# Demodulation as four side-by-side products and a fold, with woven experts and spread weight pieces

## What is computed

```python
ys = y * scale                                    # scale = 1/sqrt(512)
d = rsqrt(einsum('bi,io->bo', ys * ys, weight * weight) + EPS)
x = x + einsum('bsi,io->bso', x * ys[:, None, :], weight) * d[:, None, :]

shared = silu(xf @ w1) * (xf @ w3) @ w2           # hidden size 1024
s = sigmoid(concat([xf, tf]) @ router_W)
_, topk_idx = top_k(s + router_bias, 2)           # gates from s, normed over the two
h = gelu(einsum('nc,ech->enh', xf, W1e), approximate=False)
y = einsum('enh,ehc->enc', h, W2e)                # 8 experts, hidden size 512
out = x + (shared + einsum('ne,enc->nc', combine, y)) / 3
```

## Time and profile before

| | us |
|---|---|
| time, median of 3 runs | 1148.37 |
| lowest and highest of them | 1056.49, 2671.32 |
| time of the profiled execution | 1060.37 |
| its span, first to last instruction | 1058.6 |
| PE busy | 1031.7 |
| DVE busy | 505.7 |
| ACT busy | 292.0 |
| POOL busy | 332.0 |

### The profile page before, as it was taken

One profiled execution on the slowest core, in us unless ns is written; L12 is line 12 of the kernel. 1 busy time (PEld: TensorE's weight loads), 2 busy tenths in 40 slices (PEclk: granted clock), 3 DMA queues, 4 the chain that ended last, 5 costly groups with the idle time before them and its releaser, 6 DMA issues.

```text
span 1058.6 us, 14641 instructions
## 1 busy us (share of the span) xinstructions
PE 1031.7 (97%) x4712; PEld 842.4 (80%) x4712; DVE 505.7 (48%) x833; ACT 292.0 (28%) x461; POOL 332.0 (31%) x390
## 2 busy tenths in 40 slices
PE   9999999999999999999999998999999999999996
PEld 7888788787888888888888886788788787778874
DVE  4555556668323333243222215555555555555553
ACT  3222442322212212222121113332333233223321
POOL 0000000001223434343323301555455545545543
PEclk8999999999999999999999999999999999999998
DMA  5666688778877677886824777999779999999964
GB/s 171 199 215 223 239 285 260 261 274 278 273 238 263 193 268 241 264 276 201 291 79 108 211 226 193 218 226 221 152 139 191 225 220 226 221 219 222 230 120 80
DMA packets 133146, 228.61 MB, mean 216 GB/s; under 512 B 28912, under 2 KB 83840, under 8 KB 124992
## 3 DMA queue, kind: packets, MB, share of 16 engines
q1 hardware_dynamic: 60256, 144.05, 42.9%
q0 software_dynamic: 31360, 64.12, 26.7%
q10 hardware_dynamic: 41472, 19.68, 8.1%
HBM read 112.85 MB, written 98.38 MB: 200 GB/s over the span
## 4 chain that ended last, share of the span: by engine, by line
PE 69%; DMA 17%; issue 4%; DVE 4%; SPq 2%; POOL 1%; ACT 1%; ACTq 1%; POOLq 0%; DVEq 0%
PE banks L539 11%; PE banks L540 10%; PE banks L541 10%; PE banks L477 6%; PE banks L479 6%; PE banks L478 6%; DMA we_d<-ehl 6%; DMA we<-we_d 4%; PE banks L491 3%; PE banks L493 3%; PE banks L492 3%; PE banks L416 3%; PE banks L417 2%; PE banks L418 2%; DMA xs_d<-xrow,sadr 2%
## 5 line engine op out<-in xcount | busy, mean ns | idle before, releaser
L477 PE MATMUL banks<-xh,w 128*128 128x512 f32 x512 | 199.6, 390 | 0.6 <-DVE xl L738 0.6
L478 PE MATMUL banks<-xl,w 128*128 128x512 f32 x512 | 199.2, 389 | 0.0
L479 PE MATMUL banks<-xh,w 128*128 128x512 f32 x512 | 199.2, 389 | 0.0
L1200 POOL DMA_INDIRECT out<-ys,slot x71 | 124.6, 1754 | 187.2 <-DVE ys L1098 98.0
L807 DVE SCALAR_TENSOR_TENSOR gm<-sil,banks 128x512 f32<-128x512 f32 x64 | 43.9, 686 | 236.3 <-ACT sil L620 236.3
L1091 DVE TENSOR_TENSOR hidtl<-hidt,hidth 128x512 fp32r<-128x512 f32 x71 | 49.1, 692 | 173.8 <-ACT hidth L697 173.8
L539 PE MATMUL banks<-we,hidth 128*128 x284 | 113.6, 400 | 10.6 <-issue 9.0
L1186 POOL DMA_DIRECT2D xg<-xs_d x136 | 100.1, 1106 | 60.6 <-DVE xgt L1072 49.0
L620 ACT ACTIVATE sil<-banks 128x512 f32<-128x512 f32 x64 | 38.1, 595 | 281.8 <-PE banks L479 281.7
L539 PE MATMUL banks<-we,xgth 128*128 x284 | 111.3, 392 | 3.0 <-issue 3.0
L477 PEld LDWEIGHTS banks<-xh,w 128*128 128x128 f32 x512 | 96.1, 188 | 20.9 <-issue 1.1
(11 more groups left out here) (173 smaller groups left out, 1519.1 us busy)
## 6 DMA issues: line engine op xcount, KB each, us to landing
we_d<-ehl SPq DMA_DIRECT2D x32, 1024.0 KB, 7.3
we<-we_d SPq DMA_DIRECT2D x48, 512.0 KB, 6.0
hturn<-hid ACTq DMA_DIRECT2D x284, 64.0 KB
xg<-xs_d POOLq DMA_DIRECT2D x136, 128.0 KB
eraw<-expert_w SPq DMA_DIRECT2D x32, 512.0 KB, 5.6
x1t_d<-x1t SPq DMA_DIRECT2D x8, 1024.0 KB, 8.8
xin<-x1t_d SPq DMA_DIRECT2D x8, 1024.0 KB, 9.0
x_d<-x1tok SPq DMA_DIRECT2D x32, 256.0 KB, 6.3
```

The source lines that it names most:

```text
L477: pe.matmul(ps[hc % 2][:, :], w_hi, xh[:, j, c, :], start=(c == 0), stop=False)
L478: pe.matmul(ps[hc % 2][:, :], w_hi, xl[:, j, c, :], start=False, stop=False)
L479: last = pe.matmul(ps[hc % 2][:, :], w_lo, xh[:, j, c, :], start=False, stop=(c == DC - 1))
L1200: pool.indirect_dma_start(out[:, :], IO(slot[:, t, 0:1], 0), ys[:, t % RING, :], None, compute_op=ALU.add).then_inc(added[t % 2], 16)
```

## The change

**Beginning.** The sixteen products of 4 columns become four products of 512 columns: the weights are now the squared modulation of one chunk, widened from 4 to 32 columns with zeros, and the squared weight matrix streams through. The four chunks go to four groups of 32 columns of the array and leave their partial sums in four groups of 32 partitions. DVE copies the 128 x 512 result out of PSUM, and four products of 4 columns with a 0/1 matrix `fold` add the four groups and turn the result. The fold stands in the last chunk of `first_linear`, behind eight of its twelve products. `cnd` is loaded by ACT's queue, ahead of the x loads, and no more by POOL's.

```diff
@@ tiles
+        modwide = sb("modwide", [DC, Q], FP32, 168)
+        modsq = modwide[:, :, 0:BATCH]
+        fold = sb("fold", [BATCH], FP32, 168.5)
+        dpart = sb("dpart", [D], FP32, 170)
-        hturn = sb("hturn", [RING, SUB, P], FP32, 160)
+        hturn = sb("hturn", [RING, SUB, P], FP32, 128)
-        hidth = sb("hidth", [2, DC, P], FP32R, 132)
+        hidth = sb("hidth", [2, DC, P], FP32R, 160)
@@ tensor, demodulation
+                for c in range(DC):
+                    last = pe.matmul(dpart_ps[c * Q:(c + 1) * Q, :], modwide[:, c, :], w0sq[:, c, :], start=True, stop=True)
+                last.then_inc(dpart_done, 1)
+
+            def demodulation_sum():
+
+                pe.wait_ge(dpart_moved, 2)
                 for o in range(DC):
-                    for c in range(DC):
-                        last = pe.matmul(misc_ps[:, o * BATCH:(o + 1) * BATCH], w0sq[:, c, o * P:(o + 1) * P], modsq[:, c, :],
-                                         start=(c == 0), stop=(c == DC - 1))
+                    last = pe.matmul(misc_ps[:, o * BATCH:(o + 1) * BATCH], dpart[:, o * P:(o + 1) * P], fold[:, :], start=True, stop=True)
                 last.then_inc(misc_done, 1)
@@ vector
+            dve.wait_ge(small_in, 64)
+            dve.tensor_reduce(fold[:, :], ident.rearrange("p (c b) -> p b c", c=DC)[:, 0:BATCH, :], AX.X, ALU.add).then_inc(dpart_moved, 1)
             for c in range(DC):
                 scaled_low(1, c)
-            dve.wait_ge(small_in, 64)
+                if c == 1:
+                    dve.wait_ge(dpart_done, 1)
+                    dve.tensor_copy(dpart[:, :], dpart_ps).then_inc(dpart_moved, 1)
```

```diff
     if isinstance(n, int) and n < 2:
-        half, m = HC // 2 * n, hc
-    elif hc % 2 == 0:
-        half, m = HC // 4 * (n + 2), hc // 2
+        steps, half = ((1, 3, 5, 7), (0, 2, 3, 5))[n], 2 * n
     else:
+        steps, half = (0, 1, 3, 4, 6, 7), 3 * n - 2
+    if hc not in steps:
         return None
+    m = steps.index(hc)
```

```diff
@@ tensor
             pe.wait_ge(tables_done, 3)
+            look_up(0)
+            up(NBLK - 1, HC - 1, 1)
+            down(NBLK - 1, HC - 2)
             pe.wait_ge(gm_done, HC * NBLK - 1 + 2)
-            look_up(0)
+            matmul1(0)
             down(NBLK - 1, HC - 1)
             pe.wait_ge(gm_done, HC * NBLK + 2)
-            for t in range(TILES + LAG):
-                if t < TILES:
+            for t in range(1, TILES + LAG):
+                if t < TILES - 1:
                     matmul1(t)
+                if t == TILES - 2:
+                    matmul1(TILES - 1)
@@ scalar
-            x_high_of(0)
+            x_high_of(1)
             for t in range(TILES + TURN_LAG):
-                if t + 1 < TILES:
-                    if t:
-                        act.wait_ge(mm1_done, t)
-                    x_high_of(t + 1)
                 if t < TILES:
                     hidden(t)
-                    if t == 0:
-                        act.wait_ge(o_done, SUB * NBLK)
+                if t < TURN_LAG:
+                    x_high_of(t + 2)
+                if t < TILES - 1:
                     move_h(t)
+                if t == TURN_LAG:
+                    act.wait_ge(o_done, SUB * NBLK)
                 if t >= TURN_LAG:
                     h_high_of(t - TURN_LAG)
+                if t == TILES - 1:
+                    move_h(t)
+                if TURN_LAG <= t < TILES - 2:
+                    x_high_of(t + 2)
```

More of the change, by code:

```diff
@@ L169, in shared_moe_kernel @@
         rank_ps = bank[0]
+        dpart_ps = bank[5]
         h_ps, y_ps = bank[2:4], bank[6:8]
@@ L313, in _ @@
                         load_res(0)
-                    if n == 1 and hc == 3:
-                        sp.dma_start(out[TOK:TOK + PADROWS, :], padrows).then_inc(pads_in, 16)
                     if n and hc == 1:
@@ L350, in _ @@
             load_weight(0, first[0], slice(0, 1))
+            sp.dma_start(out[TOK:TOK + PADROWS, :], padrows).then_inc(pads_in, 16)
             for n in (NBLK - 2, NBLK - 1):
@@ L429, in first_linear @@
                         pe.matmul(lin_ps[o][:, :], wml[:, 0, c, o * P:(o + 1) * P], xh[:, 0, c, :], start=False, stop=False)
+                    if c == DC - 1:
+                        demodulation_sum()
                     pe.wait_ge(xl_ready, c + 1)
@@ L528, in _ @@
                     down(0, HC - 1)
-            with pe.Fori(1, NBLK // 2) as h:
+            with pe.Fori(1, NBLK // 2 - 1) as h:
                 for j in range(2):
                     shared_block(2 * h + j, j)
+            shared_block(NBLK - 2, 0)
+            for hc in range(HC - 1):
+                up(NBLK - 1, hc, 1)
+                if hc:
+                    down(NBLK - 1, hc - 1)
+                else:
+                    down(NBLK - 2, HC - 1)
             def product(ps, high, low, place, m, midway):
@@ L584, in x_high @@
                 act.activation(xh[:, j, c, :], xin[:, j, c, :], ACT.Copy, scale=scale).then_inc(xh_ready, 1)
+            act.dma_start(cnd[:, :, :], condT).then_inc(cond_in, 16)
             for c in range(DC):
@@ L588, in _ @@
             act.wait_ge(prep, 2)
-            act.activation(dtmp[:, :, :], modsq[:, :, :], ACT.Sqrt).then_inc(root, 1)
+            act.activation(dtmp[:, :, :], modsq, ACT.Sqrt).then_inc(root, 1)
             for c in range(DC):
@@ L640, in piece_high, with x_high_of @@
                     act.activation(ehl[:, j, 0], eraw[:, j, 1], ACT.Copy).then_inc(eh_ready, 1)
+            def x_high_of(t):
+                act.wait_ge(xturn_done, t + 1)
+                act.activation(xgth[:, t % 2], xgt[:, t % 2], ACT.Copy).then_inc(xgth_done, 1)
             def block_steps(n, j, turn, pieces=True):
                 for hc in range(HC):
+                    if turn is None and hc == HC - 1:
+                        x_high_of(0)
                     gate(n, hc)
@@ L659, in _ @@
                     w2_high(1 + hc // 2)
[L660 to L663, removed]
+                piece_high(0, hc)
             block_steps(1, 1, NBLK // 2 + 1)
@@ L729, in _ @@
             dve.memset(zeros[:, :].bitcast(FP32), 0.0).then_inc(zeros_done, 1)
+            then(dve.memset(modwide[:, :, :], 0.0))
             dve.wait_ge(cond_in, 16)
@@ L1024, in _ @@
                     choose(1)
[L1025 to L1028, removed]
+                piece_low(0, hc)
             for hc in range(HC):
@@ L1057, in _ @@
                         piece_low(2 * h + j, hc)
[L1058 to L1062, removed]
             def turn_x(t):
@@ L1078, in take_x @@
                 dve.tensor_tensor(xgtl[:, t % 2], xgt[:, t % 2], xgth[:, t % 2].bitcast(FP32), ALU.subtract).then_inc(xgt_done, 1)
+            for n in (NBLK - 2, NBLK - 1):
+                for hc in range(HC):
+                    block_step(n, hc, n % 2, n < NBLK - 1)
+                    if hc == 0:
+                        output(n - 1)
+                    if n == NBLK - 1 and hc == HC - 2:
+                        turn_x(0)
+                        turn_x(1)
+                        take_x(0)
+            for t in range(2):
+                take_x(t + 1)
+                turn_x(t + 2)
             def turn_h(t):
@@ L1115, in _ @@
                     scatter_waits()
-                if t > LAG:
+                if LAG < t < TILES - 1:
                     take_y(t - LAG - 1)
-                if t + 1 < TILES:
+                if 2 <= t < TILES - 1:
                     take_x(t + 1)
-                if t + 2 < TILES:
+                if 2 <= t < TILES - 2:
                     turn_x(t + 2)
@@ L1124, in _ @@
                     take_h(t - TURN_LAG)
+                if t >= TILES - 1:
+                    take_y(t - LAG - 1)
         @block.gpsimd
@@ L1152, in row_free @@
                 pool.wait_ge(xrow_out[i % XB], 16 * K * (i // XB + 1))
-            pool.dma_start(cnd[:, :, :], condT).then_inc(cond_in, 16)
             pool.wait_ge(tables_done, 3)
```

10 lines of the change are left out of this document (2 added, 8 removed).

## The result

| | before | after |
|---|---|---|
| median time, us | 1056.25 (8 runs) | 1044.36 (8 runs) |
| span of the profiled execution | 1058.6 | 1050.3 |
| PE busy | 1031.7 | 1025.0 |

The ratio after to before is 0.9914, with a 95% interval of 0.9891 to 0.9937: 9 us faster, 7 to 11.5. That is clear of noise and within the two per cent that the forecast gave 0.91. The forecast was 1045, by 13.3 us off.

The account below looks back on a forecast made before the run. PE, busy 1031.7 of 1058.6 us, was taken to bound the kernel. Gains of 5.3 (beginning), 2.4 (pieces), 3.1 (into the experts) and 2.5 (end) summed to 13.3 us, giving 1045 us, range 1041 to 1051 (chance 0.60).

Parts of the forecast that it names:

- The first linear product: Kernel start: with `cnd` on ACT's queue the warm-up ends last; gain 0.56 us, never more.
- The demodulation: In the first linear layer: fewer PE records gain 2.3 us, the clock staying high 2.4 more.
- the whole beginning: From kernel start through the demodulation: 0.56 + 2.3 + 2.4 = 5.3 us gained.
- The pieces: Weight pieces moved to blocks 2 to 5: PE's waits for `output` shrink, gain 2.4 us, bounds 0 and 3.0.
- Into the experts: From the last-but-one `down` to `matmul2(0)`: 19.6 us instead of 22.7, gain 3.1.
- The tiles: The 71 expert tiles: cyclic order on ACT and DVE unchanged, so their holes stay; no gain forecast.
- Rival 1: Blocks 2 to 5: added piece traffic slows POOL's row scatters, output scatters start late; 1055 us, chance 0.13.
- the fifth `take_y`: In the experts on DVE: would find its buffer full if output scatters slip; room 10 us, then 7.
- A hole at tile 6: Sign of being wrong: PE holes at tiles 1 to 6 of the experts.
- `xg` more than 43 us behind the last `store_x1`: Before the experts, sign of being wrong: `xg` issued this late, with POOL's wait for block 7's rows gone.
- The end: Last tiles: PE gains up to 4.8 us, POOL's scatters follow; gain 2.5, between 0 and 4.8.
- Rivals 2 to 4: Still slower scatters, 1078 (0.08); low clock stays or groups don't overlap, 1048 (0.12); both ends at best, 1039 (0.07).

Follow-up runs that it names:

- fold_x4: Changed kernel with the fold's four products done four times over; `linear(1)` came 16.7 us behind the first linear product, 3.7 more than in the changed kernel.
- begin_only: Kernel before with the new beginning alone (four side-by-side products, fold, `cnd` on ACT's queue); ratio to before 0.9954.
- old_pieces: Changed kernel with the weight pieces placed as before, eight in each of blocks 0 and 1, four in each of 2 to 5; ratio to before 0.9925.
- old_end: Changed kernel with the order of work at the end as before; ratio to before 0.9905.
- warm14: Changed kernel with 14 warm-up products of zeros in place of 20; span of its profile 1057.9 us.
- before_again: Kernel before, unchanged, run for a second profile; span 1051.9 us.
- y_between: Changed kernel with DVE's `take_y` between `turn_h` and `take_h` in its last steps; ratio to before 0.9901.
- last_free: Changed kernel with the last output scatter on its own semaphore, not waiting for the scatter two tiles before; ratio to before 0.9912.
- combo: Changed kernel with `store_out(7)` ahead of weight load 4's parts, 14 warm-up products and the last scatter on its own semaphore; ratio to before 0.9887.
- pair_first: Changed kernel with POOL loading tiles 8 and 9 ahead of its wait for `store_out(7)`; ratio to before 0.9878.

## Why the prediction was right, and where its steps were not

Three of the four steps came as reasoned. That the time came within 1 us of 1045 is luck in part: the forecast's base, 1058.5 us between the profiled and the lowest time, was 3.9 above the mean of the executions that the ratio uses (1054.6), and its gain of 13.3 was some 4 above the measured 9. The two misses cancel. By the means of the table's rows the end brought 0.1 us for 2.5, the tiles took 2.7 back, and the stretch with the pieces brought 1.4 more than forecast. The 2.7 are less than two executions of one kernel differ in that stretch.

**The first linear product:** right that the warm-up ends last and caps the gain. Its length varied by 1.2 us between executions with the time at which the clock rose (7.64 us in the first profile, 6.98 before), more than the 0.56 at stake. So in the first profile the step gained next to nothing (9.43 for 9.48 us), in the second 1.3.

**The demodulation:** forecast 1.0 for the four products and 1.1 for the fold; 1.00 and 0.79. The four column groups did run side by side, with the switches of tiling mode inside, as the logits' row had it. The clock held, and fold_x4 shows that it was the long sparse stretch that had cost it. From the first linear product to `linear(1)` 4.7 us were forecast and 4.6 to 4.7 measured. For the whole beginning the forecast was 5.3, and measured were 4.8 to 6.0, and 4.9 by begin_only's ratio.

**The pieces:** the waits for `outst` vanished whole. I had left 0.6 us of the second; forecast 2.4, measured 2.6 against old_pieces and 3.5 to 4.2 against before. About 1 us of the latter came with the new beginning: begin_only has the old pieces, and its waits for `outst` sum to 2.1 us, not 3.0.

**Into the experts:** `matmul2(0)` was put at 19.6 us; it came at 19.9 and 19.2, behind ACT's three times four DMAs, whose ends were put at 9.5, 14.9 and 18.2 or 18.7 and came at 8.9, 14.2 and 18.3 in the first profile.

**The tiles:** "the cyclic order on ACT and DVE is the old one, so the 71 tiles' holes stay" is the sentence that failed. The order was the same, but its supply wasn't: POOL loads tiles 8 and 9, and then 10 and 11, behind its wait for `store_out(7)`. Rival 1 had the mechanism and the place where it starts, the row scatters: DMA share forecast 0.90, measured 0.88 in block 5; POOL's wait for block 7's rows was 21.8 us, and is now 5.0 to 7.5 in eight profiles, 11.0 in old_end and none in warm14. But I priced its room at the fifth `take_y`, 7 us, and looked past what stands between on the same queue. The room for the row tiles ends some 2 to 6 us behind `matmul2(0)`. PE's side moved 11 us earlier while the store moved 4.4 in the first profile. In after, that cost 2.97 us of hole and 2.9 of low clock; in warm14 12.8 and more. A hole at tile 6 was one of the forecast's own signs of being wrong, and `xg` more than 43 us behind the last `store_x1` was part of another (before 43.2, now 43.9 and 45.6, from its first issue). The forecast's time stood it since one of the two profiles of the changed kernel has no such hole, and the other's costs 6 us.

**The end:** forecast 2.5, measured about nothing (old_end). The mechanism was named, scatter 70 behind the landing of scatter 68. Mis-sized was the distance between the two: I took 5 to 6 us, though the rows of before show 1053.41 - 1046.53 = 6.9. Measured were 7.3 and 6.9: the landing came 4.7 us behind the start of the scatter, and POOL issued the next one 2.6 us later in the first profile. So scatter 70 went at 24.9 and 24.8 us behind `matmul1(69)`, not 23.2. The 25.8 that it was compared with was itself in part chance: it is 23.8 in before_again. PE's new order also starts `matmul2(66)` 6.4 and 7.0 us behind `matmul1(69)` instead of 2.7, and with it scatter 66 went at 11.7 to 12.2 instead of 8.5. y_between moved that one too little to tell what it is worth; taking the last wait away brought the end forward (last_free).

**Rivals.** Rivals 2 to 4 did not occur. Rival 1's slip of the chain from `xg` to `store_out(7)` did in one execution, of the kernel with a shorter warm-up (1059.7 us, against 1055 forecast for it), by the tighter room above and not by the fifth `take_y`.

## What to carry to other kernels

When work is pulled forward on the bounding engine, list for every other queue what it must still do before the next operand, in program order, and how many us of room each link has then; a wait that cost nothing can be the next bound. At the end of a kernel follow the last result through to its landing: 3 us of PE there were worth next to nothing, and one semaphore wait was worth 2 in the profiles, too little for the ratio to show. And compare at least two profiles of each kernel before a hole is explained: here the same code differed by 9 us of span.

## What the runs showed of the hardware

The granted clock fell while PE was busy without a gap, during 16 products with 4 columns each: 6.8 us at 1.2 GHz in both profiles of before and 3.4 us in fold_x4. It also fell at some holes of 1.8 to 3.5 us among dense products (1.82 us in combo, then 3.4 us low; 2.97 in after, then 6.8), and not at others (2.44 us in pair_first, 3.16 in after at `matmul2(0)`). So a hole cost its length and sometimes 1.7 to 3 us more, half of the time that PE worked at the low clock.

Four fp32 products of 512 columns in four groups of 32 columns took 1.00 us, the tiling switches included, as sixteen of 128 columns did (1.01). A scatter that adds 128 rows to the output landed 4.4 to 4.9 us behind its start at the end of after.
